# A routed transformer branch on one core: smaller pieces and another order in its preparation, mask, softmax and MLP

## The chip, the cores and the metric

One core of one Trainium2 chip. The metric is the device time of one execution in microseconds, of which the median of several runs is given. Lower is better.

## What is computed

Two layers on x of 2048 x 128, all in float32. Each is `x + s * silu(g)`, with s an attention and g a second branch, both of the layer-normed x. The change is in layer 0's second branch, the routed one, and in what prepares it. Cut to what matters:

```python
def _L0_ffn_ref(x, attention_mask, position_ids, router_w, router_b, wq, wk, wv, wo, w1, w2, ln1, ln2):
    weights = (x @ router_w)[..., 0] + router_b[0]
    k = int(CAP * s)                                  # 256 of 2048
    topv, topi = jax.lax.top_k(weights, k)
    sel_mask = (weights > topv[:, -1][:, None]).astype(x.dtype)
    kc = k - 1                                        # 255
    sel_idx = jnp.sort(topi[:, :kc], axis=1)
    x_sel, pos_sel, w_sel = x[bidx, sel_idx], position_ids[bidx, sel_idx], weights[bidx, sel_idx]
    m_sel = m[bidx[:, :, None], sel_idx[:, :, None], sel_idx[:, None, :]]   # 512 x 512 mask, indices clamped
    hn = rmsnorm(x_sel, ln1)
    q, kk, v = rope(heads(hn @ wq), pos_sel), rope(heads(hn @ wk), pos_sel), heads(hn @ wv)   # 16 heads of 8
    a = jax.nn.softmax(q @ kk.T / sqrt(8) + m_sel, axis=-1)
    x1 = x_sel + (a @ v).reshape(...) @ wo
    x2 = x1 + jax.nn.gelu(rmsnorm(x1, ln2) @ w1) @ w2
    proc = x2 * w_sel[..., None]
    out = jnp.zeros_like(x).at[bidx, sel_idx].set(proc)
    return out + x * (1.0 - sel_mask)[..., None]
```

The first attention (16 heads of 8, relu weights) and the whole second layer are not touched.

## The kernel before

Each stage is a block in which the five engines have a program of their own, written out by hand and tied by counting semaphores. An engine runs its instructions in the order written and stops at each `wait_ge`. At the end of a block all engines meet, and the next block starts. The stages are `prepare` (to 44.8 us in the profile), `routed0` (to 120.8 us), `attention0`, `between` and `attention1`.

`prepare` loads and norms x, turns it, makes the router's weights as a row and a column, projects q, k and v, and counts for each token how many weigh more. VectorE compares a weight column with the weight row for t = 0 to 15 (lines 258 and 261). ScalarE counts the first seven of these (line 295) and copies v after the first four. GpSimd makes rows of equal weights (lines 198 and 202) and TensorE adds the counts (lines 353 and 355). In between, `high(n)` on ScalarE copies a projected piece of q or k in TensorE's own rounding (line 287), and `low(n)` on VectorE makes the rest of it (line 252). `HIGHS_AFTER` and `LOWS_AFTER` say behind which t; n = 0 to 3 is q, n = 4 to 7 is k. SyncE stores each of the four parts to DRAM, 1 MB apiece, when its pieces are there (line 166), and the block can't end before these have landed. The first attention reads q and k back from there.

`routed0` gathers the chosen tokens by matmuls with one-hot rows, made by VectorE from the ranks (line 877), last 12 row tiles first and then the four tiles of the 512 tokens that the mask covers (`T_ORDER`). GpSimd adds up the 12 later tiles (`tails`, lines 865 to 868), since the mask takes all later tokens as its last one. VectorE squares and norms the gathered rows (lines 889 to 901), TensorE turns and projects them. The mask is taken by columns (`mask_columns`, line 1063, copies on line 1010) and then by rows (line 1129), and copied to `mask_sel` (line 941). Scores of four heads at a time (`score`) are masked by VectorE (line 955, two halves of 128 slots a head), exponentiated by ScalarE (line 1026), turned by TensorE (line 1148) and weighed (line 1157). Behind that, in order: the reciprocal of the sums spread to all columns (line 965) and turned (1172), `place` of the one-hot rows (turned tiles, line 1077, copied on lines 1036 and 978), `oT` (969), output projection (1179), x1 (971), norm, w1 (1193), gelu (1040), w2 (1199), x2 (981), the scatter (1208) and silu (1044). Banks of PSUM are assigned by hand in `PLACE_BANK` and `TURN_BANK`. An activation function that is not in the loaded table costs ScalarE a table load (ACT_TABLE_LOAD).

Of the kernel before, what the change touches and what calls it, by code (L numbers as in the profile page):

```python
# [78 lines left out]
def prepare(nc, a, sh):  # L79

    with ExitStack() as ctx:
# [63 lines left out]
        HIGHS_AFTER = {2: range(NC, 2 * NC)}  # L145
        LOWS_AFTER = {1: range(0, 2), 2: range(2, NC), 10: range(NC, 2 * NC)}
# [561 lines left out]
def routed0(nc, a, sh):  # L708


    with ExitStack() as ctx:
# [106 lines left out]
        PLACE_BANK = [0, 1, 2, 3, 2, 3, 5, 6]  # L818
# [27 lines left out]
        def _(pool):  # L846
# [17 lines left out]
            pool.wait_ge(ranked, T - MT)  # L864
# [6 lines left out]
        def _(dve):  # L871
# [65 lines left out]
            for i in range(RES):  # L937
                nc.vector.tensor_scalar(qm[:, i, :], bank[6][:, 0:SLOTS], head_rows[:, i:i + 1], None,
                                        ALU.mult).then_inc(qm_done, 1)
            dve.wait_ge(mask_taken, 1)  # L940
            link(nc.vector.tensor_copy(mask_sel[:, :, 0:SEL],
                                       bank[7].rearrange("p (s k) -> p s k", s=NS)[:, :, 0:SEL]))
# [7 lines left out]

            for n in range(H):
                if n % GH == 0:
                    dve.wait_ge(scored, n // GH + 1)
                for s in range(NS):
                    last = nc.vector.tensor_tensor_reduce(
                        out=prob[:, head(n), s, :], in0=bank[n % GH][:, s * SLOTS:(s + 1) * SLOTS],
                        in1=mask_sel[:, s, :], scale=-1.0, scalar=3.0e38, op0=ALU.add, op1=ALU.min,
                        accum_out=top[:, head(n), s:s + 1])
                last.then_inc(masked, 1)
                if n % GH == GH - 1:  # L960
                    for m in range(n - GH + 1, n + 1):
                        if not by_act(m):
                            take_probs(m)
            dve.wait_ge(exped, H)
            nc.vector.reciprocal(hn[:, :, :].rearrange("p s (h j) -> p s h j", j=HD0),
                                 total[:, :, :].unsqueeze(3).to_broadcast([P, NS, H, HD0])).then_inc(share_ready, 1)
# [8 lines left out]
            take_turned(1, bank[7])  # L975
# [5 lines left out]
            link(nc.vector.tensor_tensor(proc[:, :, :], bank[4][:, 0:NS * D].rearrange("p (s d) -> p s d", s=NS),  # L981
# [15 lines left out]
        def _(act):  # L997
# [10 lines left out]
            for n in range(2):  # L1008
                act.wait_ge(cols_taken, n + 1)
                nc.scalar.copy(mask_cols[:, 2 * n:2 * n + 2, :], sh.psum[:, 2 * n:2 * n + 2, 0:SLOTS])\  # L1010
                    .then_inc(cols_out, 1)
            act.wait_ge(qk_turned, 1)
            nc.scalar.copy(kT[:, :], bank[7][:, 0:SLOTS]).then_inc(kT_done, 1)

# [7 lines left out]
            for n in range(H + 2):  # L1022
# [7 lines left out]
                if n >= 2 and by_act(n - 2):  # L1030
                    take_probs(n - 2)
# [1131 lines left out]
```

## Time and profile before

| | us |
|---|---|
| Median of 3 runs | 1413.13 (1411.38 to 1413.79) |
| The profiled execution | 1410.19 |
| Its span, first to last instruction | 1408.2 |
| Preparation / routed branch | 0 to 44.8 / to 120.8 |
| TensorE busy | 1313.0 (93%) |
| VectorE busy | 1015.9 (72%) |
| ScalarE busy | 749.8 (53%) |
| GpSimd busy | 691.9 (49%) |
| Mean granted TensorE clock | 0.982 of full |

Times in the rows are microseconds from the first instruction of the profiled execution. PE is TensorE's matmuls, PEld its weight loads, DVE VectorE, ACT ScalarE, POOL GpSimd, SPq SyncE's queue. A float32 matmul shows as two instructions. Several equal instructions in a row are one row with their count (x4), and its duration runs from the first's start to the last's end. The bracket tells how long the engine was idle before and who released it. An end that overlaps the next start by about 0.1 us is usual.

### The profile page before, as it was taken

The numbers are of one execution on the slowest core, as the hardware profiler recorded it, in microseconds if no ns is written. First come the engines' busy times: TensorE is split into PE (matmuls) and PEld (weight loads), VectorE is DVE, ScalarE is ACT, GpSimd is POOL, SyncE is SP. The second block draws the span as 40 slices with busy tenths as digits, with TensorE's granted clock in tenths as the row PEclk, the third lists the DMA queues.
The fourth block names the chain that finished last, engine by engine and source line by source line (L and its number), as shares of the span: only waits on it lengthen the run. The fifth ranks groups of instructions, "written<-read, shape, count | busy, mean of one in ns | idle before, by whom it ended". The sixth has DMA issues, their size and how long they took to land.

```text
span 1408.2 us, 25489 instructions
## 1 busy us (share of the span) xinstructions
PE 1313.0 (93%) x9902; PEld 674.9 (48%) x9902; DVE 1015.9 (72%) x1495; ACT 749.8 (53%) x1200; POOL 691.9 (49%) x527
## 2 busy tenths in 40 slices
PE   5778999999999987989999999999999999999897
PEld 3654222222222245555555655555555555555554
DVE  7666888888888875776766766766766666766768
ACT  5275777877777774334444444444344344344343
POOL 4301060100100010558678678677677677777671
PEclk9799999999999999999999999999999999999999
DMA  2511320000000000000000000000000000000000
GB/s 98 160 74 51 111 47 1 1 1 1 2 1 2 2 1 1 1 1 1 1 1 1 1 1 1 1 1 0 1 1 1 1 1 1 1 1 1 1 16 16
DMA packets 18166, 21.50 MB, mean 15 GB/s; under 512 B 7785, under 2 KB 15873, under 8 KB 16513
## 3 DMA queue, kind: packets, MB, share of 16 engines
q1 hardware_dynamic: 18048, 19.88, 4.6%
q8 instruction: 81, 1.33, 0.4%
q14 instruction: 37, 0.30, 0.1%
HBM read 14.63 MB, written 5.24 MB: 14 GB/s over the span
## 4 chain that ended last, share of the span: by engine, by line
PE 43%; DVE 11%; ACT 3%; issue 1%; POOL 1%; DVEq 0%; POOLq 0%; ACTq 0%
PE psum L1810 13%; PE psum L1788 12%; DVE part_max L1952 4%; PE psum L1731 4%; DVE inv L1973 4%; PE psum L1791 3%; ACT prob L1895 3%; PE psum L1769 2%; PE psum L1718 2%; PE psum L1757 2%; PE psum L1709 1%; DVE z L1976 1%; PE psum L1711 1%; PE psum L1710 1%; PE psum L1736 1%
## 5 line engine op out<-in xcount | busy, mean ns | idle before, releaser
L1698 POOL TENSOR_TENSOR acc<-acc,prob 128x1024 f32<-128x1024 f32 (+3 forms) x250 | 492.8, 1971 | 87.4 <-ACT prob L1895 57.6
L1895 ACT ACTIVATE prob<-psum 128x1024 f32<-128x1024 f32 (+1 forms) x320 | 283.3, 897 | 353.8 <-PE psum L1791 346.4
L1952 DVE TENSOR_REDUCE part_max<-psum 128x2 f32<-128x1024 f32 (+2 forms) x320 | 336.7, 1063 | 170.0 <-PE psum L1731 85.6
L696 DVE TENSOR_SCALAR w<-psum 128x512 f32<-128x512 f32 x472 | 304.7, 686 | 59.0 <-PE psum L553 46.6
L647 ACT ACTIVATE w<-psum 128x512 f32<-128x512 f32 x552 | 294.2, 600 | 85.4 <-PE psum L553 84.8
L573 PE MATMUL psum<-w,v_cols 128*32 128x512 f32 x2048 | 274.1, 608 | 0.0
L1810 PE MATMUL psum<-prob,v_pair 128*64 128x512 f32 (+3 forms) x1280 | 250.2, 532 | 0.7 <-POOL prob L1666 0.7
L1788 PE MATMUL psum<-q_hi,k_hi 64*128 64x512 f32 (+3 forms) x640 | 139.0, 430 | 30.4 <-DVE part_max L1952 21.5
L1810 PEld LDWEIGHTS psum<-prob,v_pair 128*64 128x64 f32 x1280 | 87.4, 137 | 145.2 <-issue 134.2
L1731 PE MATMUL psum<-k_hi,q_hi 64*128 64x512 f32 (+3 forms) x640 | 132.5, 411 | 6.0 <-DVE part_max L1952 4.4
L1788 PE MATMUL psum<-q_lo,k_hi 64*128 64x512 f32 (+3 forms) x640 | 119.1, 368 | 0.0
L1788 PE MATMUL psum<-q_hi,k_lo 64*128 64x512 f32 (+3 forms) x640 | 119.1, 368 | 0.0
L1791 PE MATMUL psum<-max_rows,ones_r 64*128 64x512 f32 (+3 forms) x640 | 118.7, 366 | 0.0
L1973 DVE RECIPROCAL inv<-psum 128x512 f32<-128x512 f32 x31 | 103.9, 3352 | 16.5 <-PE psum L1757 16.5
L553 PEld LDWEIGHTS psum<-q_rows,k_rows 32*128 32x128 f32 x768 | 40.3, 181 | 154.0 <-ACT w L647 148.1
L397 POOL TENSOR_SCALAR xa<-xa,rstd_j,shift_j 128x128 f32<-128x128 f32 x16 | 6.9, 449 | 209.0 <-DVE shift_j L389 209.0
L1666 POOL TENSOR_SCALAR_AFFINE_SELECT prob<-prob 128x256 f32<-128x256 f32 x128 | 53.3, 423 | 110.9 <-ACT prob L1895 110.1
L553 PE MATMUL psum<-q_rows,k_rows 32*128 32x512 f32 x768 | 101.6, 493 | 0.1
L1788 PEld LDWEIGHTS psum<-q_hi,k_hi 64*128 64x128 f32 x640 | 61.4, 188 | 78.0 <-DVE part_max L1952 47.4
L1731 PEld LDWEIGHTS psum<-k_hi,q_hi 64*128 64x128 f32 x640 | 61.2, 187 | 77.6 <-issue 40.8
L1694 POOL TENSOR_TENSOR acc<-prob 128x1024 f32<-128x1024 f32 x23 | 54.9, 2385 | 43.2 <-ACT prob L1895 41.4
L573 PEld LDWEIGHTS psum<-w,v_cols 128*32 128x32 f32 x2048 | 40.6, 108 | 63.8 <-ACT w L647 53.5
(301 smaller groups left out, 1411.3 us busy)
## 6 DMA issues: line engine op xcount, KB each, us to landing
q_rows<-q_dram SPq DMA_DIRECT2D x12, 256.0 KB
k_rows<-k_dram SPq DMA_DIRECT2D x3, 1024.0 KB
q_dram<-parts SPq DMA_DIRECT2D x2, 1024.0 KB, 4.2
k_dram<-parts SPq DMA_DIRECT2D x2, 1024.0 KB, 6.6
x<-in_L_attn_x SPq DMA_DIRECT2D x4, 256.0 KB, 4.0
mask<-in_L_ffn_attention_mask SPq DMA_DIRECT2D x1, 1024.0 KB, 6.0
x_high<-q_dram SPq DMA_DIRECT2D x4, 256.0 KB
x_low<-k_dram SPq DMA_DIRECT2D x1, 1024.0 KB
```

What stands on the lines that cost most here:

```text
L553: last = nc.tensor.matmul(pair_bank[n % RING][i], k_rows[group][rows, kt * P:(kt + 1) * P], q_rows[group][rows, qc * C:(qc + 1) * C], star ...
L573: last = nc.tensor.matmul(out_bank[turn % 2][h * VW:(h + 1) * VW, :], v_cols[group][:, kt, h, :], w[:, s % WR, h, :], start=(kt == 0), sto ...
L647: nc.scalar.activation(w[:, s % WR, 2 * m + i, :], pair_bank[n % RING][i], ACT.Relu)\
L696: nc.vector.tensor_scalar(w[:, s % WR, 2 * m + 1, :], pair_bank[n % RING][1], 0.0, None, ALU.max)\
L1698: nc.gpsimd.tensor_tensor(sums, sums, prob[:, s % PR, :, q0:C], ALU.add).then_inc(summed, 1)
L1731: last = nc.tensor.matmul(to[:, m, 0:n], q_hi[HALF[m], i * P:(i + 1) * P], k_hi[hp % 2][HALF[m], c * C:c * C + n], start=True, stop=not di ...
L1788: nc.tensor.matmul(to[:, m, q0:C], left[HALF[m], keys], right[HALF[m], at], start=n == 0, stop=False)
L1791: last = nc.tensor.matmul(to[:, m, q0:C], ones_r[HALF[m], :], max_rows[HALF[m], at], start=False, stop=True)
L1810: last = nc.tensor.matmul(out_bank[HALF[m], q0:C], v_pair[hp % 2][:, kt, HALF[m]], prob[:, s % PR, m, q0:C], start=kt == 0, stop=kt == (qc ...
L1895: nc.scalar.activation(prob[:, s % PR, :, q0:C], unit_both[n % RING][:, :, q0:C], ACT.Exp, scale=SCALE)\
L1952: nc.vector.tensor_reduce(part_max[:, :, i, c], unit_both[n % RING][:, :, 0:cols], AX_X, ALU.max)\
L1973: nc.vector.reciprocal(inv[:, :], side_bank).then_inc(inv_done, 1)
```

## The change

- k's high parts are copied behind ScalarE's second count (was: third), its low parts made behind VectorE's eighth compare (was: eleventh).
- GpSimd starts the sums of later rows when all 16 one-hot tiles exist (was: the 12 later ones).
- The mask: kT is copied ahead of the mask's columns, these are copied one by one, and the rows are made in two halves in two banks, with the first scores between them. The first four heads are masked by halves.
- The softmax sums are inverted at 32 columns and then spread by a copy.
- ScalarE runs a square root on a spare element behind the last probabilities, so that the table is loaded there.
- Two `place` calls go ahead of the share's transposes, two behind the output projection with the rest; banks follow.
- w1, gelu and w2 go by halves; w2's two row halves sum into two banks.

```diff
-        HIGHS_AFTER = {2: range(NC, 2 * NC)}
-        LOWS_AFTER = {1: range(0, 2), 2: range(2, NC), 10: range(NC, 2 * NC)}
+        HIGHS_AFTER = {1: range(NC, 2 * NC)}
+        LOWS_AFTER = {1: range(0, 2), 2: range(2, NC), 7: range(NC, 2 * NC)}
...
-        PLACE_BANK = [0, 1, 2, 3, 2, 3, 5, 6]
+        PLACE_BANK = [0, 1, 2, 3, 0, 1, 7, 6]
...
-            pool.wait_ge(ranked, T - MT)
+            pool.wait_ge(ranked, T)
@@ def _(dve) @@
-            dve.wait_ge(mask_taken, 1)
-            link(nc.vector.tensor_copy(mask_sel[:, :, 0:SEL],
-                                       bank[7].rearrange("p (s k) -> p s k", s=NS)[:, :, 0:SEL]))
+            MASK_BANK = [bank[7], bank[6]]
...
+            for s in range(NS):
+                dve.wait_ge(mask_taken, s + 1)
+                link(nc.vector.tensor_copy(mask_sel[:, s, 0:SEL], MASK_BANK[s][:, 0:SEL]))
+                dve.wait_ge(scored, 1)
+                for n in range(GH):
+                    last = mask_scores(n, s)
+                    if s == NS - 1:
+                        last.then_inc(masked, 1)
             for n in range(H):
-                if n % GH == 0:
-                    dve.wait_ge(scored, n // GH + 1)
-                for s in range(NS):
-                    last = nc.vector.tensor_tensor_reduce(
...
-                last.then_inc(masked, 1)
+                if n >= GH:
+                    if n % GH == 0:
+                        dve.wait_ge(scored, n // GH + 1)
+                    mask_scores(n, 0)
+                    mask_scores(n, 1).then_inc(masked, 1)
...
-            nc.vector.reciprocal(hn[:, :, :].rearrange("p s (h j) -> p s h j", j=HD0),
-                                 total[:, :, :].unsqueeze(3).to_broadcast([P, NS, H, HD0])).then_inc(share_ready, 1)
+            link(nc.vector.reciprocal(total[:, :, :], total[:, :, :]))
+            nc.vector.tensor_copy(hn[:, :, :].rearrange("p s (h j) -> p s h j", j=HD0),
+                                  total[:, :, :].unsqueeze(3).to_broadcast([P, NS, H, HD0])).then_inc(share_ready, 1)
...
-            take_turned(1, bank[7])
+            take_turned(1, bank[5])
...
-            link(nc.vector.tensor_tensor(proc[:, :, :], bank[4][:, 0:NS * D].rearrange("p (s d) -> p s d", s=NS),
+            link(nc.vector.tensor_tensor(proc[:, :, :], sh.psum[:, 4:4 + NS, 0:D],
@@ def _(act) @@
-            for n in range(2):
-                act.wait_ge(cols_taken, n + 1)
-                nc.scalar.copy(mask_cols[:, 2 * n:2 * n + 2, :], sh.psum[:, 2 * n:2 * n + 2, 0:SLOTS])\
-                    .then_inc(cols_out, 1)
             act.wait_ge(qk_turned, 1)
             nc.scalar.copy(kT[:, :], bank[7][:, 0:SLOTS]).then_inc(kT_done, 1)
+            for c in range(MT):
+                act.wait_ge(cols_taken, c + 1)
+                nc.scalar.copy(mask_cols[:, c, :], bank[c][:, 0:SLOTS]).then_inc(cols_out, 1)
...
+            nc.scalar.activation(idle[:, :], sh.ones[:, 0:1], ACT.Sqrt)
             act.wait_ge(share_spread, 1)
...
-            act.wait_ge(hidden, 1)
-            nc.scalar.activation(gate[:, :], sh.psum[:, 0:2, :].rearrange("p b c -> p (b c)"), ACT.Gelu_apprx_tanh)\
-                .then_inc(gated, 1)
+            for n in range(2):
+                act.wait_ge(hidden, n + 1)
+                nc.scalar.activation(gate[:, n * C:(n + 1) * C], bank[2 + n], ACT.Gelu_apprx_tanh).then_inc(gated, 1)
@@ def _(pe) @@
             for c in range(MT):
-                last = mask_columns(c, MT - 1)
-                if c % 2:
-                    last.then_inc(cols_taken, 1)
+                mask_columns(c, MT - 1).then_inc(cols_taken, 1)
...
-            pe.wait_ge(cols_out, 2)
...
+            pe.wait_ge(cols_out, MT)
+            mask_slots(0)
             score(0)
+            pe.wait_ge(qm_done, RES)
+            mask_slots(1)
...
                 if n == 2:
-                    pe.wait_ge(qm_done, RES)
+                    pe.wait_ge(masked, GH)
...
+            for u in range(2):
+                place(u)
             pe.wait_ge(share_ready, 1)
...
-            for u in range(NC):
-                place(u)
             pe.wait_ge(oT_done, 1)
...
-            for u in range(NC, NC + 3):
+            for u in range(2, NC + 3):
                 if u == NC:
-                    pe.wait_ge(placed_by_act, NC)
-                if u == NC + 2:
-                    pe.wait_ge(share_out, 1)
+                    pe.wait_ge(placed_by_act, 2)
                 place(u)
-            turn_hn(1, bank[7])
+            turn_hn(1, bank[5])
             place(NC + 3)
+            pe.wait_ge(placed_by_act, NC)
...
-                last = nc.tensor.matmul(bank[f // 2][:, (f % 2) * SLOTS:(f % 2 + 1) * SLOTS], w1[:, f * P:(f + 1) * P],
+                last = nc.tensor.matmul(bank[2 + f // 2][:, (f % 2) * SLOTS:(f % 2 + 1) * SLOTS], w1[:, f * P:(f + 1) * P],
...
-            last.then_inc(hidden, 1)
-            pe.wait_ge(gated, 1)
-            for s in range(NS):
-                for f in range(FT):
+                if f % 2:
+                    last.then_inc(hidden, 1)
+            for f in range(FT):
+                pe.wait_ge(gated, f // 2 + 1)
+                for s in range(NS):
```

`mask_scores(n, s)` is the masking instruction of line 955, and `mask_slots(s)` the matmuls of line 1129 for one s, into bank 7 or 6.

## Rows read from the trace of the kernel before

**Rows 1.** SyncE's waits from 0 to 180 us: total, times, longest.

```profile
SPq L81 <- DMA k_dram<-parts: 6.2, 1, 6.2
```

**Rows 2.** Timeline, end of the preparation: start, us, engine, line, op, out<-in [idle before].

```profile
29.00 0.58 ACT L299 COPY v<-psum 128x512 f32<-128x512 f32 x1
...
30.66 1.39 DVE L261 TENSOR_SCALAR_CACHE_REDUCE prob<-g,xa 128x1152 bf16<-128x1152 f32 x1
...
31.62 2.07 ACT L287 CAST parts<-psum 128x512 fp32r<-128x512 f32 x4
...
33.72 4.50 SPq L166 DMA_DIRECT2D k_dram<-parts  x2
...
35.19 2.47 DVE L252 TENSOR_TENSOR parts<-psum,parts 128x512 fp32r<-128x512 f32 x4
...
42.53 0.17 PE L355 MATMUL psum<-minus_b,equal 128*128 128x1 bf16 x1
...
44.86 0.18 DVE L874 TENSOR_TENSOR rank<-counts,before 128x16 f32<-128x16 f32 x1 [4.54 <-PEq L81]
```

**Rows 3.** Timeline, one-hot rows, gather and GpSimd's adds.

```profile
46.01 8.86 PEld L1052 LDWEIGHTS psum<-xa,onehot 128*128 128x128 f32 x56 [3.40 <-DVE onehot L877]
...
50.65 3.48 POOL L865 TENSOR_TENSOR prob<-onehot 128x1536 f32<-128x1536 f32 x1 [1.54 <-DVE onehot L877]
...
50.75 3.53 DVE L877 TENSOR_SCALAR onehot<-iota,rank 128x256 f32<-128x256 f32 x1
...
54.21 1.80 POOL L866 TENSOR_TENSOR prob<-prob 128x768 f32<-128x768 f32 x1
...
56.89 0.76 POOL L868 TENSOR_TENSOR prob<-prob 128x256 f32<-128x256 f32 x1
...
57.79 0.44 DVE L884 COPY xs<-psum 128x274 f32<-128x274 f32 x1 [0.72 <-PE psum L1052]
...
58.82 0.17 DVE L893 TENSOR_SCALAR square<-square 128x2 f32<-128x2 f32 x1
```

**Rows 4.** Lines 877 and 1931, VectorE: duration ns min/median/max, first and last start.

```profile
L877 DVE TENSOR_SCALAR onehot<-iota,rank x16: 333/342/3530, 45.3 to 56.1; 128x256 f32<-128x256 f32 x16
...
L1931 DVE TENSOR_TENSOR xa<-xa,g x3: 692/1732/1916, 1334.1 to 1381.0; 128x512 f32<-128x512 f32 x3
```

**Rows 5.** Timeline, from the mask's columns to the first exponential.

```profile
67.77 0.58 ACT L1010 COPY w_heads<-psum 128x512 f32<-128x512 f32 x1 [0.28 <-PE psum L1063]
...
68.25 0.38 ACT L1013 COPY kT<-psum 128x256 f32<-128x256 f32 x1
...
72.50 0.69 DVE L941 COPY mask_sel<-psum 128x510 f32<-128x510 f32 x1 [4.73 <-PE psum L1129]
...
74.53 0.51 ACT L1026 ACTIVATE prob<-prob,top 128x256 f32<-128x256 f32 x1 [5.90 <-DVE top L955]
```

**Rows 6.** Timeline, from the softmax's end to x2.

```profile
95.16 1.75 DVE L965 RECIPROCAL hn<-total 128x256 f32<-128x256 f32 x1 [1.04 <-ACT prob L1026]
...
95.88 0.58 ACT L1019 COPY mask<-psum 128x512 f32<-128x512 f32 x1 [0.27 <-PE psum L1148]
...
98.34 1.97 PE L1077 MATMUL psum<-ident,onehot 128*128 128x128 f32 x16
...
100.79 0.42 DVE L971 TENSOR_TENSOR x_sel<-psum,xs 128x256 f32<-128x256 f32 x1 [1.82 <-PE psum L1179]
...
101.10 1.28 ACT L1038 ACT_TABLE_LOAD   x1
...
107.17 1.02 ACT L1040 ACTIVATE w_heads<-psum 128x1024 f32<-128x1024 f32 x1 [3.27 <-PE psum L1193]
...
110.33 0.42 DVE L981 TENSOR_TENSOR proc<-psum,x_sel 128x256 f32<-128x256 f32 x1 [2.86 <-PE psum L1199]
```

**Rows 7.** Windows at the first attention's start: length, TensorE busy (instructions), clock, DMA share, GB/s.

```profile
122.00:123.00 1.00, 0.77 (x4) 0.60 0.16 16
...
128.00:129.00 1.00, 1.00 (x8) 0.50 0.69 172
```

More of the change, by code:

```diff
@@ L949, in take_probs, with mask_scores @@
                     .then_inc(probT_by_dve, 1)
-            for n in range(H):
-                if n % GH == 0:
-                    dve.wait_ge(scored, n // GH + 1)
-                for s in range(NS):
-                    last = nc.vector.tensor_tensor_reduce(
-                        out=prob[:, head(n), s, :], in0=bank[n % GH][:, s * SLOTS:(s + 1) * SLOTS],
-                        in1=mask_sel[:, s, :], scale=-1.0, scalar=3.0e38, op0=ALU.add, op1=ALU.min,
-                        accum_out=top[:, head(n), s:s + 1])
-                last.then_inc(masked, 1)
+            def mask_scores(n, s):
+                return nc.vector.tensor_tensor_reduce(
+                    out=prob[:, head(n), s, :], in0=bank[n % GH][:, s * SLOTS:(s + 1) * SLOTS],
+                    in1=mask_sel[:, s, :], scale=-1.0, scalar=3.0e38, op0=ALU.add, op1=ALU.min,
+                    accum_out=top[:, head(n), s:s + 1])
+            for s in range(NS):
[6 more added lines that the diff above has]
+                        last.then_inc(masked, 1)
+            for n in range(H):
+                if n >= GH:
[3 more added lines that the diff above has]
+                    mask_scores(n, 1).then_inc(masked, 1)
                 if n % GH == GH - 1:
@@ L1123, in score, with mask_slots @@
                 last.then_inc(scored, 1)
-            pe.wait_ge(cols_out, 2)
-            pe.wait_ge(kT_done, 1)
-            for s in range(NS):
-                for c in range(MT):
-                    last = nc.tensor.matmul(bank[7][:, s * SLOTS:(s + 1) * SLOTS], mask_cols[:, c, s * P:(s + 1) * P],
-                                            rows(c), start=(c == 0), stop=(c == MT - 1))
-            last.then_inc(mask_taken, 1)
+            def mask_slots(s):
+                for c in range(MT):
+                    last = nc.tensor.matmul([bank[7], bank[6]][s][:, 0:SLOTS], mask_cols[:, c, s * P:(s + 1) * P],
+                                            rows(c), start=(c == 0), stop=(c == MT - 1))
+                last.then_inc(mask_taken, 1)
+            pe.wait_ge(kT_done, 1)
+            pe.wait_ge(cols_out, MT)
+            mask_slots(0)
             score(0)
+            pe.wait_ge(qm_done, RES)
+            mask_slots(1)
             def wait_probs(n):
@@ L1192, in _ @@
             for f in range(FT):
-                last = nc.tensor.matmul(bank[f // 2][:, (f % 2) * SLOTS:(f % 2 + 1) * SLOTS], w1[:, f * P:(f + 1) * P],
+                last = nc.tensor.matmul(bank[2 + f // 2][:, (f % 2) * SLOTS:(f % 2 + 1) * SLOTS], w1[:, f * P:(f + 1) * P],
                                         hnT[:, :], start=True, stop=True)
-            last.then_inc(hidden, 1)
-            pe.wait_ge(gated, 1)
-            for s in range(NS):
-                for f in range(FT):
-                    last = nc.tensor.matmul(bank[4][:, s * D:(s + 1) * D],
+                if f % 2:
[3 more added lines that the diff above has]
+                for s in range(NS):
+                    last = nc.tensor.matmul(bank[4 + s][:, 0:D],
                                             gate[:, f * SLOTS + s * P:f * SLOTS + (s + 1) * P], w2[:, f, :],
```

## The prediction

> **What bounds the kernel now.** I read the page first: TensorE is busy for 93% of the span, but that is mostly the two attentions, which the edit does not touch. The edited code is all in the first 121 us. The chain of waits is of no use there (it is followed back only into the second attention), so I went to the timeline, stretch by stretch, and asked what each engine's first instruction after an idle time had waited for. Up to 121 us every stage hands its result to the next and nothing overlaps the attention behind it, so a microsecond taken off this chain is a microsecond off the kernel, as long as the attention keeps its pace.
>
> Four places matter. (1) The preparation ends when its last engine does. TensorE's last count ends at 42.70, but the next stage starts at 44.86: SyncE sits 6.2 us on the landing of the stores to k_dram, and all wait for it [rows 1, 2]. (2) In the one-hot stretch VectorE loses time to GpSimd: the 14th one-hot row takes 3.53 us where the median is 0.34; it starts 0.1 us after GpSimd's first add (50.65) and ends 0.15 us after it (54.13) [rows 3, 4]. (3) Scores wait for the mask: TensorE, ScalarE's copies, TensorE again, one VectorE copy of both halves, and only then the first masked score [rows 5]. (4) Behind the softmax come a reciprocal of 1.75 us, sixteen placing transposes between the last weighing and the output projection, a table load that the root waits for, and a gelu of 1.02 us in one piece [rows 6].
>
> **k's stores.** The high copies of k move from behind ScalarE's third count to behind its second, which with its value copy ends at 29.58. The four copies, 2.07 us, then end near 31.65 in place of 33.69, if their projection is done by then. VectorE's low parts go ahead of three compares: the eighth compare ends near 32.05, the low parts take 2.47, so they end at 34.5 instead of 37.66 [rows 2]. By the later store the landing moves 3.1 us; if the two share the bandwidth and the first sets the pace, 2.0. SyncE's wait began at 38.2, behind its last issue, so the landing was at 44.4; it comes to between 41.3 and 42.4, before TensorE's 42.70. TensorE's counts wait for GpSimd's equality rows and for compares that end when they did. So the landing stops being last and TensorE becomes last, and behind it stands the barrier, which took 0.4 us after the landing (44.4 to 44.86) [rows 1, 2]. The next stage starts near 43.05: **1.8 us gained**, bounds 1.2 (landing late) and 2.1.
>
> **The sums of later rows.** I keep the clock of before here. With GpSimd quiet the last three one-hots pass by 51.6, and TensorE, which was busy with the first 56 gather matmuls up to 54.9 anyway, finishes the other eight near 56.1, so that the copy of the gathered rows starts there and not at 57.79: 1.7 us seem won. But GpSimd's four adds now start at 51.7, not at 50.65, and take as long as before, 7.0 us (the third under 0.9): to 58.7 [rows 3]. VectorE's next work, the squares, reads two operands in SBUF. What such an instruction does beside a GpSimd add is shown by line 1931: 0.69 us alone, 1.73 and 1.92 while adds run [rows 4]; and one VectorE instruction gets through at each gap between adds, as the 14th one-hot did [rows 3]. So: gathered rows copied from PSUM 56.1 to 56.5; the first square waits for the second add, 57.06; the second square for the third, 57.95; the small scaling of the squares for the fourth, about 58.9. Before it started at 58.82 [rows 3]. **Gain 0**, bounds -0.2 and +1.2. The +1.2 is the case in which squares are not held: then the small scalings alone are held, and the sum matmul, which needs the fourth add at 58.7, stands ahead of the turned hn in TensorE's queue and caps it.
>
> The Trainium skill (SBUF — State Buffer, section "SBUF: two separate sides") says that the port pair which VectorE and GpSimd share is locked for a whole instruction, also by a VectorE instruction with two SBUF inputs beside a GpSimd one that reads SBUF. By that rule the squares are held and this edit gives 0, where the one-hots alone would promise 1.7; the trace of line 1931 agrees (0.69 against 1.92 us).
>
> **The mask by halves.** kT is copied first, while TensorE still makes the last columns; the four column copies of 256 take 0.38 each (as kT), and only the last one stands behind the last column, where a copy of 0.58 and then kT's stood: ready near 68.15 instead of 68.63, gain 0.5. TensorE then takes from 68.7 to 72.5 for both halves. Now it does one, near 1.9 us, then score(0), then the other, while VectorE masks the first half under it. The last half ends near 72.9; copy 0.42, one masked score, and the first exponential starts at 73.9 instead of 74.53 [rows 5]. **0.6 gained**, bounds 0.2 and 1.1 (whether score(0) holds TensorE for its whole time). ScalarE then paces the sixteen heads as before, two exponentials of 0.5 us each; the new wait for four masked heads ahead of the third head's transposes is long met, since ScalarE needs 3 us to get there.
>
> **Softmax to scatter**, in times of before [rows 6].
> - The reciprocal has 32 columns instead of 256: 0.22 in proportion, with a fixed cost up to 0.4; the copy spread to 256 columns 0.33 to 0.42 (a one-hot row, kT's size). About 0.8 for 1.75, ready at 96.0. But TensorE has place(0) and place(1) first, half of what took 1.97, so until 96.5. The share's transposes, which came behind 96.91, start at 96.5.
> - ScalarE loads the square root's table right behind its last probability copy (96.46): 1.28, and a tiny activation of 0.2, to 97.95. Only then comes the share copy, 0.37, to 98.3. The weighing, done by 98.34 before, is done at 97.9. So the table load takes back part of what the reciprocal gave.
> - oT takes 98.3 to 98.75 and the output projection follows at once; before, all sixteen placing transposes (98.34 to 100.1, where the next matmul gets in) held TensorE. With 0.75 for the projection x1 starts at 99.55 instead of 100.79: 1.25 gained.
> - Squares are ready 1.2 later (as from 57.79 to 58.99 [rows 3]), 100.75. Before, the root stood behind a table load that ended at 102.38; that load is gone, but two placing copies of 0.5 stand ahead on ScalarE and end near 101.1. Root at 101.1 instead of 102.4: 1.3 gained.
> - w1's eight matmuls have half the number and twice the columns of w2's sixteen, which take 2.1 (gelu's end 108.19 to 110.33). The first four give their half of the gelu 1.0 sooner: it starts near 104.9, takes 0.6, the second half ends at 106.45. w2's first half runs beside it from 105.6, its second from 106.6 and 1.1 more: x2 at 107.8 instead of 110.33. **2.5 gained in all**, bounds 1.5 and 3.0. VectorE's four placing copies stay hidden beside the gelus; uncovered they would cost 0.6 each.
>
> Sum: 1.8 + 0 + 0.6 + 2.5 = 4.9. The profiled execution took 1410.19 (span 1408.2 and 2.0 around it), so it would take 1405.3. The median of the runs shown, 1413.13, is 2.9 above it; for a median I say 1413.13 - 4.9 = **1408.2**.
>
> **The rivals.**
> - Squares not held by the adds: 1.2 more, 1407.0. For it: the squares are another form than line 1931, and none stands beside an add in this trace. Against: line 1931. Chance 0.10.
> - The clock at the start of the first attention. TensorE idles before 120.9, and the granted clock is at its low level (1.2 GHz) from 122.4 to 129 [rows 7]. At most half of such a stretch is lost, about 3 us. The shifted stage may be spared it: 1405.2. Chance 0.08.
> - Half the gain: the barrier still waits for the landing of two stores back to back, or ScalarE's queue with table load and placing copies sets the end of the branch. 4.9 less 1.2 to 2.5 leaves 2.4 to 3.7, that is 1409.4 to 1410.7, and with the spread of the runs mostly within 0.2% (2.8 us, about what a measurement of this kernel can tell from no change). Chance 0.18.
> - Slower: the same low clock lasts longer. It has to give back 4.9 + 2.8 = 7.7 us, at a half lost over 15 us more at the low level in the attention's first steps, more than twice the stretch of before. For it: the work in front of it moves by 5 us. Against: TensorE is busy all through. With 20 us more: 1418. Chance 0.04.
> - The main case keeps 0.60, its own range 1406.2 to 1410.0.
>
> Faster 0.60 + 0.10 + 0.08 = 0.78, same 0.18, slower 0.04. The range goes from the spared clock stretch, 1404.8, to the half gain with the runs' spread, 1411.4.
>
> **What would show it.** The routed stage starts near 43.0 with TensorE's count as the last of the preparation; the adds end near 56.9 and a square of over 0.5 us stands among them; the first exponential comes 2.4 us before 74.53; the square root's table load stands ahead of the share copy; two gelus; the attention's first matmul near 116.0. Wrong would be: squares of 0.29 us beside adds, SyncE still last, a share copy that isn't delayed, or another length of the low clock behind the attention's start.

## The result and the profile after

| | before | after |
|---|---|---|
| Median of 5 runs each, same comparison, us | 1411.38 (1410.73 to 1413.79) | 1403.77 (1402.92 to 1404.42) |
| Ratio | | 0.9942 [0.9928, 0.9955] |
| Profiled execution / its span | 1410.19 / 1408.2 | 1403.8 / 1401.9 |
| Mean granted TensorE clock | 0.982 | 0.986 |
| Attention's first matmul (L553) | 120.86 | 116.63 |

The kernel became faster, 7.6 us by the medians where 4.9 were forecast, and 1403.77 lies 1.0 below the range. The median of before was 1413.13 in three runs and 1411.38 in five, so 1.75 of the miss of 4.4 lies in the base of the sum. In the profiled executions 4.2 us were won ahead of the attention (120.86 to 116.63), 2.1 behind it, in code that the edit doesn't touch.

SyncE's waits of after [rows 1]: total, times, longest.

```profile
SPq L81 <- DMA k_dram<-parts: 6.4, 1, 6.4
SPq L81 <- PEq L81: 1.8, 1, 1.8
```

The timeline of after, end of the preparation [rows 2].

```profile
29.56 0.58 ACT L299 COPY v<-psum 128x512 f32<-128x512 f32 x1
30.02 2.07 ACT L287 CAST parts<-psum 128x512 fp32r<-128x512 f32 x4
...
32.12 3.47 SPq L166 DMA_DIRECT2D k_dram<-parts  x2
...
32.55 2.47 DVE L252 TENSOR_TENSOR parts<-psum,parts 128x512 fp32r<-128x512 f32 x4
...
43.62 0.19 PE L353 MATMUL psum<-one_b,prob 128*128 128x1 bf16 x1 [1.34 <-issue]
...
44.13 0.18 DVE L874 TENSOR_TENSOR rank<-counts,before 128x16 f32<-128x16 f32 x1 [3.24 <-PEq L81]
```

SyncE finds the stores landed at about 42.0 (its last issue ends at 35.59, then 6.4) and waits 1.8 more, for TensorE. The landing isn't last any more. But TensorE's last two counts stand behind a pause of 1.34 that nothing in the profile explains. The stage begins 0.73 earlier than before, not 1.8. A part of this arises ahead of the edit: from VectorE's first norm (L220) to its copy of the weight column (L243) after took 10.34 us and before 9.87.

The timeline of after, from GpSimd's first add to TensorE's sum of the later rows [rows 3].

```profile
50.97 3.44 POOL L865 TENSOR_TENSOR prob<-onehot 128x1536 f32<-128x1536 f32 x1 [2.59 <-DVE onehot L877]
...
54.44 0.44 DVE L884 COPY xs<-psum 128x274 f32<-128x274 f32 x1 [3.45 <-PE psum L1062]
54.49 1.81 POOL L866 TENSOR_TENSOR prob<-prob 128x768 f32<-128x768 f32 x1
54.92 1.53 DVE L889 CUSTOM_DVE_ANT_0 hn<-xs 128x128 f32<-128x128 f32 x1
56.38 0.87 POOL L867 TENSOR_TENSOR prob<-prob 128x256 f32<-128x256 f32 x1
...
56.38 0.28 DVE L889 CUSTOM_DVE_ANT_0 hn<-xs 128x128 f32<-128x128 f32 x1
...
56.70 0.57 DVE L893 TENSOR_SCALAR square<-square 128x2 f32<-128x2 f32 x1
57.31 0.20 ACT L1009 ACTIVATE root_sel<-square 128x2 f32<-128x2 f32 x1 [11.94 <-DVE square L893]
57.33 0.72 POOL L868 TENSOR_TENSOR prob<-prob 128x256 f32<-128x256 f32 x1
...
58.10 0.70 PE L1080 MATMUL psum<-prob,ones 128*128 128x256 f32 x2 [0.88 <-POOL prob L868]
```

The first square takes 1.53 us in place of 0.28 and ends just behind the second add (56.45 and 56.30). The second square follows in the same gap and isn't held. The tiny scaling is held (0.57) by the third add. The fourth add is waited for by TensorE's sum of the later rows alone (58.10), which ends before the normed rows are there to be turned (59.11), so it costs nothing here.

The timeline of after, mask [rows 5].

```profile
64.86 1.67 ACT L1022 COPY w_heads<-psum 128x256 f32<-128x256 f32 x4
...
66.67 1.53 PE L1135 MATMUL psum<-onehot,w_heads 128*128 128x256 f32 x6 [0.55 <-ACT w_heads L1022]
...
68.56 1.15 PE L1129 MATMUL psum<-kT,wo 32*128 32x256 f32 x16
...
69.64 1.56 PE L1135 MATMUL psum<-onehot,w_heads 128*128 128x256 f32 x6
...
71.67 0.42 DVE L957 COPY mask_sel<-psum 128x255 f32<-128x255 f32 x1 [0.32 <-PE psum L1135]
...
72.60 0.51 ACT L1035 ACTIVATE prob<-prob,top 128x256 f32<-128x256 f32 x1 [6.07 <-DVE top L950]
```

Both halves and score(0) stand one behind the other on TensorE, 66.67 to about 71.6.

The timeline of after, softmax's end to x2 [rows 6].

```profile
93.69 0.35 DVE L974 RECIPROCAL total<-total 128x32 f32<-128x32 f32 x1 [1.04 <-ACT prob L1035]
94.08 0.30 DVE L975 COPY hn<-total 128x256 f32<-128x256 f32 x1
...
95.01 1.28 ACT L1041 ACT_TABLE_LOAD   x1
...
96.30 0.20 ACT L1041 ACTIVATE idle<-ones 128x1 f32<-128x1 f32 x1
96.41 0.35 ACT L1043 COPY share<-psum 128x256 f32<-128x256 f32 x1
...
98.03 0.42 DVE L981 TENSOR_TENSOR x_sel<-psum,xs 128x256 f32<-128x256 f32 x1 [0.80 <-PE psum L1191]
...
99.42 0.22 ACT L1048 ACTIVATE root_sel<-square 128x2 f32<-128x2 f32 x1
99.66 1.28 ACT L1051 ACT_TABLE_LOAD   x1
...
103.36 0.60 ACT L1051 ACTIVATE w_heads<-psum 128x512 f32<-128x512 f32 x1 [2.42 <-PE psum L1204]
...
106.10 0.42 DVE L991 TENSOR_TENSOR proc<-psum,x_sel 128x256 f32<-128x256 f32 x1 [1.59 <-PE psum L1211]
```

The reciprocal and its copy take 0.7 for 1.75. The share copy waits for the table load, as forecast: TensorE delivered the turned share at about 95.5, and ScalarE takes it at 96.41.

In a table, each stage from its own start, so that a shift ahead of it doesn't count:

| stage, us | before | after | gain | forecast |
|---|---|---|---|---|
| VectorE's first norm to L874 (k's stores) | 34.01 | 33.20 | 0.8 | 1.8 |
| L874 to the copy of hnT (one-hots, adds, norm) | 16.49 | 15.60 | 0.9 | 0 |
| rotation to the first exponential (mask) | 11.53 | 11.22 | 0.3 | 0.6 |
| exponentials to the reciprocal (heads) | 20.63 | 21.09 | -0.5 | 0 |
| reciprocal to x2 | 15.17 | 12.41 | 2.8 | 2.5 |
| attention's first matmul to the end | 1287.34 | 1285.27 | 2.1 | 0 |

The attention's gain goes with the clock. The heads' loss of 0.5 isn't explained: both executions have one stretch of 3.4 us at the low level among the heads. Windows of after at the attention's start [rows 7]: length, TensorE busy (instructions), weight loads, VectorE, ScalarE, GpSimd, granted clock, DMA share, GB/s.

```profile
119.00:120.00 1.00, 0.90 (x8) 0.37 (x10) 1.00 (x3) 0.99 (x3) 1.00 (x3) 0.90 0.12 49
120.00:121.00 1.00, 1.00 (x8) 0.00 (x0) 0.84 (x2) 0.34 (x1) 1.00 (x2) 0.50 0.57 172
...
122.00:123.00 1.00, 1.00 (x12) 0.20 (x8) 0.78 (x2) 0.78 (x2) 0.37 (x1) 0.50 1.16 262
```

Summed over such windows, the low level (0.50, that is 1.2 GHz of 2.4) lasts 3.4 us here and 6.8 before. Behind 110 us as a whole it lasts 29.9 us before, in stretches at 122, 562, 794, 1002, 1108, 1316 and 1402, and 22.6 after, at 119, 788, 997, 1102, 1311 and 1396. These are the same places in the code, some 5 us earlier; the one at 562 is missing and the first is half as long. Two more stretches of after, around 788 and 893 (length, TensorE busy, clock, DMA share, GB/s):

```profile
786.00:787.00 1.00, 0.00 (x0) 1.00 0.00 0
...
789.00:790.00 1.00, 1.00 (x6) 0.50 0.00 0
```

```profile
891.00:892.00 1.00, 0.00 (x0) 1.00 0.00 0
...
894.00:895.00 1.00, 1.00 (x10) 1.00 0.00 0
```

In both TensorE idles for a little under 2 us and then works on. The clock falls behind the first idle time and not behind the second.

### The profile page after: what moved, and what is told of

Read it like the earlier page. It is cut to its first block, busy times and chain, and to the rows that moved or that the text cites. A ratio compares the mean times of both kernels' runs of the same rounds, so it can differ in the third digit from the quotient of the medians.

```text
span 1401.9 us, 25496 instructions
## 1 busy us (share of the span) xinstructions
PE 1309.4 (93%) x9902; PEld 672.0 (48%) x9902; DVE 1012.3 (72%) x1497; ACT 750.4 (54%) x1204; POOL 692.1 (49%) x527
## 4 chain that ended last, share of the span: by engine, by line
PE 43%; DVE 11%; ACT 3%; issue 1%; POOL 1%; DVEq 0%; POOLq 0%; ACTq 0%
PE psum L1822 13%; PE psum L1800 12%; DVE part_max L1964 4%; PE psum L1743 4%; DVE inv L1985 4%; PE psum L1803 3%; ACT prob L1907 2%; PE psum L1781 2%; PE psum L1730 2%; PE psum L1769 2%; PE psum L1721 1%; DVE z L1988 1%; PE psum L1723 1%; PE psum L1722 1%; PE psum L1748 1%
## 5 line engine op out<-in xcount | busy, mean ns | idle before, releaser
L553 PEld LDWEIGHTS psum<-q_rows,k_rows 32*128 32x128 f32 x768 | 40.0, 181 | 153.8 <-ACT w L647 146.3
L553 PE MATMUL psum<-q_rows,k_rows 32*128 32x512 f32 x768 | 101.2, 493 | 0.1
(303 smaller groups left out, 1404.7 us busy)
```

Of the source, the lines that this page charges most:

```text
L553: last = nc.tensor.matmul(pair_bank[n % RING][i], k_rows[group][rows, kt * P:(kt + 1) * P], q_rows[group][rows, qc * C:(qc + 1) * C], star ...
```

## The experiments

Each is the kernel after with one edit or none (sums_vector_filled and sums_scatter_filled have more), 4 to 10 runs of it beside 10 to 26 of before; ratios are to these runs of before, with a 95% interval. Stages and spans are of its profiled execution, compared with the table's.

**1. after_again.** The kernel after once more.

> The changed kernel once more, unchanged. Of the 6.4 us between the two profiled executions 4.2 are there at the first attention's start; the other 2.1 appear where the granted clock is at its low level in one and not in the other (3.9 instead of 6.6 us of it at the attention's start, none instead of 3 us near 562). Theory A, the low stretches fall by chance: this execution shows them at other places or of other lengths, and the span differs from 1401.9 by 1 to 3 us. Theory B, they belong to the kernel: same places within 1 us, span within 0.5 us of 1401.9. Median for both: 1403.8 give or take 1.

1404.71, ratio 0.9963 [0.9951, 0.9976], span 1402.6, the attention's first matmul at 115.70. The same kernel gains 6.0 here. The preparation took 32.08 for 33.20, with no pause of TensorE ahead of the last counts where after has 1.34, and the low level behind 110 us lasted 30.1, as before. So the branch gives 5.2 us and the rest 0.4.

**2, 3. delay_short, delay_long.** GpSimd clears a spare tile behind the branch, so that the attention starts 1.5 or 3.0 us later.

```diff
+            pool.wait_ge(combined, NC)
+            nc.gpsimd.memset(onehot[:, 0:8, :], 0.0)
+            nc.gpsimd.memset(onehot[:, 8:9, :], 0.0)     # delay_long: 8:16
```

> The changed kernel with GpSimd kept at work for about 1.7 us more at the end of the routed branch, all engines waiting. If the rest of the kernel is a fixed length, the time rises by 1.7 us (1405.5). If the low clock stretches behind it depend on the moment at which the stages begin, their lengths or places change and the rise is off by 1 us or more either way.

> The same with about 3.3 us. Fixed length: 1407.1. Dependence on the moment: off by 1 us or more, and not by the same amount as with the short delay. A longer idle time of TensorE may also lengthen the low stretch at the attention's start: then both are above their sums.

1407.92 (0.9978 [0.9967, 0.9989]) and 1408.04 (0.9978 [0.9969, 0.9987]). The expectations had 1405.5 and 1407.1 for a rest of fixed length, so both runs are above, and twice the delay cost the same. Between x2 and the attention the two profiles have 12.01 and 13.50 us (10.53 in after), so the delay is paid in full there. But delay_short had two low-level stretches among its heads (22.96 us) and delay_long none (20.22), and behind 110 us the low level lasted 41.1 against 33.3 us: the stretches differ by more than the 1.5 us between the two. In both profiles the low level at the attention's start lasted 10.2 us, where the eleven others without spare matmuls have 3.4 or 6.8. So a longer idle time of TensorE ahead of the attention went with a longer low stretch, which the second expectation had named.

**4. k_stores_as_before.** k's parts at their old places.

```diff
-        HIGHS_AFTER = {1: range(NC, 2 * NC)}
-        LOWS_AFTER = {1: range(0, 2), 2: range(2, NC), 7: range(NC, 2 * NC)}
+        HIGHS_AFTER = {2: range(NC, 2 * NC)}
+        LOWS_AFTER = {1: range(0, 2), 2: range(2, NC), 10: range(NC, 2 * NC)}
```

> Only the placing of k's high and low parts goes back to that of before. My sum had 1.8 us for it; the two profiles show the routed stage's start 0.7 earlier, with all of the preparation 0.6 later from its first load on, so 1.3. Theory of the sum: the routed stage starts 1.3 later (near 45.4 or, counted from the first count on, the same), SyncE again waits about 6 us for the landing. Rival: the landing is hidden or not by other things and the start moves by less than 0.5 us.

1406.11, 0.9967 [0.9957, 0.9976]; preparation 33.92. Its timeline and SyncE's waits:

```profile
43.44 0.18 PE L353 MATMUL psum<-one_b,prob 128*128 128x1 bf16 x1 [1.70 <-issue]
```

```profile
SPq L81 <- DMA k_dram<-parts: 6.2, 1, 6.2
...
SPq L81 <- PEq L81: 0.2, 1, 0.2
```

Here the pause is longest, 1.70, and costs nothing: the landing ends behind it. What stands ahead of the edit varies too (9.3 to 10.5 us from the first norm to the weight column), so I count from the weight column (L243) to L874. With late stores that took 24.14 us (before, pause 0.78) and 24.16 (here, 1.70). With early stores it took 21.5 to 21.6 in the six profiles without a pause and 22.3 to 22.9 in the eight with one of 0.8 to 1.3. So this edit is worth 2.6 us without the pause and 1.3 to 1.8 with it, in one and the same code.

**5. sums_early.** GpSimd's adds start with twelve one-hots, as before.

```diff
-            pool.wait_ge(ranked, T)
+            pool.wait_ge(ranked, T - MT)
```

> Only GpSimd's start goes back: it adds when 12 one-hot tiles exist. My prediction gave this edit 0; the profiles show 0.9 to 1.0 us from the stage's start to the turned hn. Theory of the profile: the hn is ready 0.9 later and so is everything behind. Rival, that the gain came from the clock rising 4.0 instead of 5.6 us after the stage's start: then the time stays the same within 0.3, since the clock rises as early here.

1405.18, 0.9962 [0.9952, 0.9971]. L874 to hnT took 16.48, as before (16.49) and 0.9 over after, though the clock rose as early as in after (4.0 us behind L874): the rival is out, and the term is this one wait.

It isn't always 0.9. Of the eleven profiles in which GpSimd's adds wait for all 16 tiles, eight took 15.6 to 15.7; there the clock rose 4.0 to 5.6 us behind L874. In delay_short, reciprocal_spread and gelu_in_one_loaded it rose at 7.0 to 7.4, the gathered rows were copied 11.8 to 12.0 us behind L874 (after: 10.31), and the stage took 16.3. Timeline of delay_short, where lines stand 3 lower:

```profile
56.55 0.28 DVE L892 CUSTOM_DVE_ANT_0 hn<-xs 128x128 f32<-128x128 f32 x1
...
56.88 0.57 DVE L896 TENSOR_SCALAR square<-square 128x2 f32<-128x2 f32 x1
```

The squares missed the gap behind the second add. The first was held by the third add (55.75 to 56.48), the second passed in the gap behind it, and the scaling was held by the fourth. The edit then gives 0.2, near the forecast.

**6. sums_on_vector.** The four adds move to VectorE.

```diff
-            pool.wait_ge(ranked, T)          # and the four adds on nc.gpsimd
+            dve.wait_ge(ranked, T)           # on VectorE, behind the threshold
+            link(nc.vector.tensor_tensor(tails[:, :, :], onehot[:, MT:MT + 6, :], onehot[:, MT + 6:T, :], ALU.add))
...
             dve.wait_ge(gathered, 1)
```

> VectorE makes the four adds itself, in the 3.5 us that it idles between the last one-hot and the gather's end, and GpSimd does nothing then. If GpSimd's adds hold the squares (0.28 alone, 1.53 in the profile after), both squares take 0.28, the small scaling 0.17, and the turned hn comes 1.3 to 1.7 us earlier. If the holding is not the cause, no change, or a loss when the adds (about 3.1 us by the 128x512 adds of 0.69) end behind the gather.

1402.04, 0.9946 [0.993, 0.9963], span 1399.1. Timeline:

```profile
49.74 1.76 DVE L879 TENSOR_TENSOR prob<-onehot 128x1536 f32<-128x1536 f32 x1
51.53 0.96 DVE L880 TENSOR_TENSOR prob<-prob 128x768 f32<-128x768 f32 x1
...
54.46 0.29 DVE L889 CUSTOM_DVE_ANT_0 hn<-xs 128x128 f32<-128x128 f32 x1
...
55.22 0.20 ACT L1009 ACTIVATE root_sel<-square 128x2 f32<-128x2 f32 x1 [11.03 <-DVE square L893]
```

The adds cost half as long on VectorE (1.76 for 3.44), lie under the gather, and both squares take 0.29. L874 to hnT: 14.60, a whole us under after. Set beside kernels in which the clock rose at the same time the gain is 1.1 to 1.65: 1.1 here (after_again 15.72), 1.65 in sums_vector_filled (13.95 against 15.60), 1.1 in sums_scatter_filled (15.23 against 16.31). The held square was real.

**7. mask_as_before.** Column copies in pairs ahead of kT's, both halves of the mask ahead of score(0); VectorE keeps its new order.

```diff
             mask_slots(0)
-            score(0)
             pe.wait_ge(qm_done, RES)
             mask_slots(1)
+            score(0)
```

> Column copies in two pairs ahead of kT, and both halves of the mask ahead of the first scores; VectorE still masks the first four heads by halves. The profiles show 0.3 from the rope to the first exponential where my sum had 0.6, split as 0.5 for the copies and 0.1 for the halves. If the copies give 0.5 and the halves take 0.2 back, this kernel is 0.3 to 0.5 later at the first exponential (11.5 to 11.7 from the rope instead of 11.2); since only the last of four heads' first halves stands before the second, it can also be later than before (11.5). Rival: the order does nothing, 11.2.

1406.44, 0.9963 [0.9949, 0.9978]. Rotation to first exponential: 13.02, worse than before (11.53): the scores come last, and VectorE then masks four first halves (1.4 us) ahead of the second mask copy. The expectation had 11.5 to 11.7 and named a time above 11.5 as possible. This is no measure of the old code: here the halves come on VectorE alone.

**8. reciprocal_spread.** The reciprocal on 256 spread columns again.

```diff
-            link(nc.vector.reciprocal(total[:, :, :], total[:, :, :]))
-            nc.vector.tensor_copy(hn..., total...to_broadcast([P, NS, H, HD0]))
+            nc.vector.reciprocal(hn..., total...to_broadcast([P, NS, H, HD0]))
```

> Only the reciprocal goes back to 256 columns (1.75 us). Because two placings stand ahead of the share's transposes on TensorE and the table load ahead of the share copy on ScalarE, I expect only 0.4 of the 1.1 us to show at oT: 3.5 from reciprocal to oT instead of 3.1. Rival (the reciprocal is on the path with its whole length): 4.2.

1407.2, 0.9969 [0.9956, 0.9983]. Reciprocal to oT took 3.38 for 3.11, so 0.27 of 1.1 saved on VectorE reach the path (expected: 0.4); the table load holds the rest. The heads took 23.09 us, with two low stretches.

**9. no_early_sqrt.** The tiny root ahead of the share copy is left out.

```diff
-            nc.scalar.activation(idle[:, :], sh.ones[:, 0:1], ACT.Sqrt)
```

> Only the activation that loads the square root's table early is taken out. The share copy then comes 0.9 earlier, but the weighing still sets the output product, so 0.2 are won there; behind it the load stands ahead of the root once more, behind the placing copies, and costs 1.3 less the 0.4 that the root waited anyway. Sum: about 0.8 slower. Rival (ScalarE's queue was the limit, and the early load only moved the wait): no change.

1406.23, 0.9977 [0.9967, 0.9987]. Timeline:

```profile
95.17 0.37 ACT L1042 COPY share<-psum 128x256 f32<-128x256 f32 x1 [0.51 <-PE psum L1185]
...
97.50 0.42 DVE L981 TENSOR_TENSOR x_sel<-psum,xs 128x256 f32<-128x256 f32 x1 [0.80 <-PE psum L1190]
...
99.03 1.28 ACT L1047 ACT_TABLE_LOAD   x1
100.33 0.20 ACT L1047 ACTIVATE root_sel<-square 128x2 f32<-128x2 f32 x1
```

From x1 to the root 2.83 us for 1.39, but from the reciprocal to oT 2.90 for 3.11: the early load wins 1.44 and costs 0.21, 1.2 in all where 0.8 was expected. From the root to x2 it took 8.25 for 6.68. TensorE idled 2.31 us for the normed rows (after: 0.90), and a low stretch fell on w1's matmuls.

**10, 11. mlp_in_one, gelu_in_one_loaded.** One gelu for both halves of the hidden columns; the second with its table loaded ahead by a tiny gelu.

```diff
-            for n in range(2):
-                act.wait_ge(hidden, n + 1)
-                nc.scalar.activation(gate[:, n * C:(n + 1) * C], bank[2 + n], ACT.Gelu_apprx_tanh).then_inc(gated, 1)
+            nc.scalar.activation(idle[:, :], sh.ones[:, 0:1], ACT.Gelu_apprx_tanh)   # gelu_in_one_loaded only
+            act.wait_ge(hidden, 2)
+            nc.scalar.activation(gate[:, :], sh.psum[:, 2:4, :]..., ACT.Gelu_apprx_tanh).then_inc(gated, 2)
```

> Only the gelu goes back to one piece of 1024 columns (w1's and w2's orders stay). My sum had 1.2 us for the halves, the profiles show 1.25 between root and x2. Theory: root to x2 takes about 7.9 in place of 6.7, at the same clock, and everything behind comes 1.2 later. Rival: w2's new order of its own gives part of it, then less than 0.8.

> The gelu in one piece again, with a one-element gelu right behind the root so that the table is loaded there, as in the changed kernel. Theory: 8.0 from root to x2 instead of 6.7, if no low clock stretch falls into it (1.6 more if it falls on w2). Rival: most of the loss of the run before was the load's place; then under 7.3.

1408.28 (0.9976 [0.9965, 0.9986]) and 1405.14 (0.9952 [0.9937, 0.9967]). The timeline of mlp_in_one:

```profile
101.50 1.28 ACT L1050 ACT_TABLE_LOAD   x1 [4.63 <-PE psum L1204]
102.79 1.02 ACT L1050 ACTIVATE w_heads<-psum 128x1024 f32<-128x1024 f32 x1
...
103.86 3.67 PE L1211 MATMUL psum<-w_heads 128*128 128x128 f32 x16 [2.45 <-ACT w_heads L1050]
```

Root to x2 took 10.92 for 6.68, where 7.9 was expected. It measured three things at once: in this kernel the table load came behind the wait for the hidden columns (1.28), where in after it runs right behind the root (99.66), and w2's matmuls fell into the low clock (3.67 for 2.04), behind an idle time of 2.45. The second kernel has neither: root to x2 took 8.03 for 6.68, so halves are worth 1.35.

**12 to 14. filled_gaps, sums_vector_filled, sums_scatter_filled.** Spare matmuls of 512 columns, two behind the mask's second half and two behind the scatter, whose results nobody reads. The second kernel has the edit of sums_on_vector as well, the third too, but only the spare matmuls behind the scatter.

```diff
+            for _ in range(2):
+                nc.tensor.matmul(bank[7], sh.ident[:, :], sh.xnT[:, 0:C], start=True, stop=True)
```

> Two spare float32 matmuls of 512 columns (1.7 us) go into TensorE's idle time behind the mask's second half and two behind the scatter. Nothing waits for them. If idle time of TensorE brings on the low clock, the low stretches at 75.7 to 78.6 and at 119.9 to 123.9 are shorter or gone: up to 0.4 and 1.4 us. If they come on regardless, no change, or a loss of up to 0.5 where the spare matmuls end late.

> Both versions that came out below the changed kernel together: the sums on VectorE and spare matmuls in two of TensorE's gaps. The sums give 1.0 at the turned hn. If the spare matmuls keep the clock up, there is no low stretch between 70 and 85 and none at the first attention's start, again as in their own profile, and the time is near 1401 to 1402. If that profile was luck, low stretches stand there again and the time is that of the sums alone, 1402.0 to 1403.5.

> Sums on VectorE and the two spare matmuls behind the scatter, none behind the mask. If the spare matmuls keep the clock up there: no low stretch between 110 and 130 and the first steps of the attention at 1.44 us from the third on. If it was luck: a low stretch of 3.4 or 6.8 us there, as in 12 of 12 without them. Time 1401 to 1403.

1402.91 (0.995 [0.9931, 0.9968]), 1402.72 (0.9936 [0.9916, 0.9956]) and 1404.7 (0.9957 [0.9944, 0.9969]). The same windows, first of sums_vector_filled, then of sums_scatter_filled:

```profile
119.00:120.00 1.00, 1.00 (x12) 0.35 (x12) 0.68 (x2) 0.19 (x1) 1.00 (x2) 1.00 0.83 156
```

```profile
119.00:120.00 1.00, 1.00 (x8) 0.04 (x4) 0.83 (x2) 0.55 (x1) 1.00 (x2) 0.50 0.63 164
```

The spare matmuls cut TensorE's idle time ahead of the attention from 2.12 to 0.40 us. The first two profiles have no low stretch at the attention's start and looked like a cure; the third, with the same matmuls in the same gap, has one of 6.8 us. All 13 profiles without spare matmuls have such a stretch, two of three with them don't. Three profiles are too few to say that the gap ahead of the attention calls the low level.

## Why the prediction missed

**The step that failed** is the last one, from the sum to the median: "for a median I say 1413.13 - 4.9", with the clock kept as in before. The result lies 4.4 us under 1408.2. Of these 2.3 are the base (1413.13, where 71 runs of before have a mean of 1410.8). Another 1.5 are the clock: these five runs have a mean of 0.985 and the 71 have 0.9825, and a straight line through the 71 gives 0.6 us for each 0.001. The remaining 0.6 is the sum itself. In it the mechanisms held, with one exception. The step that was wrong there is "one VectorE instruction gets through at each gap between adds", which made the one-hot term 0; it measured 0.9. The ends of the range, 1404.8 and 1411.4, stand 0.4 and 0.7 outside of the rivals' own times (1405.2 and 1410.7), without a working.

**The base.** "For a median I say 1413.13 - 4.9". Three runs carried it. Over the 71 runs of before that stood beside all experiments the mean is 1410.8 (1407.65 to 1413.34), so the profiled execution's 1410.19 was the better base: 1410.19 - 4.9 = 1405.3, which I had written down and left, would have been 1.5 above the result.

**The sums of later rows: gain 0, measured 0.9.** The mechanism held up to one step. The adds started 6.84 us behind the stage's start, as forecast (51.7 - 44.86), took 7.1, and held a square. What failed is the line "one VectorE instruction gets through at each gap between adds": two did. The second square passed in the first square's gap, so the scaling waited for the third add and not the fourth. In the three profiles whose clock rose late, the squares came a gap later and the gain was 0.2. The rival "squares not held" is out. The trace agrees with the rule that I cited of the Trainium skill (SBUF — State Buffer, section "SBUF: two separate sides"), here with 1.53 against 0.28 us for the same instruction. How many get through in a gap I had read from one case.

**k's stores: 1.8, measured 0.8 and 1.9 over the whole preparation, 1.3 and 2.6 from the weight column on.** The landing came at 42.0, within the 41.3 to 42.4 forecast, and TensorE became last. Mis-sized was TensorE's end: 42.70 forecast, 43.84 measured, of which 0.58 is that everything ran later (the copy of v at 29.00 and 29.56), most of it from ahead of the edit, and 0.56 the longer pause (0.78 and 1.34). Where the pause was 0.81, nearly that of before (filled_gaps), the edit gave 1.8 from the weight column on (22.32 for 24.14), the forecast. after_again, without the pause, has 2.6. A wait that had covered an irregular pause was taken away, and the pause came out. My bounds had no term for it.

**The mask: 0.6, measured 0.3.** The copies gave 0.5 (they end 5.15 us behind the rotation's start, 5.63 before). The halves cost 0.2 instead of giving 0.1: TensorE needs 5.0 us from the first half to the end of the second, with score(0) and two pauses of 0.33 between, where I had 4.7. That is the low bound that I named, "score(0) holds TensorE for its whole time".

**Softmax to scatter: 2.5, measured 2.8.** oT 0.3, x1 1.0, root 0.2, MLP 1.25; the forecast had 0.2, 1.05 more, 0.05 more, 1.2. The table load took back most of the reciprocal, as costed. The next activation starts at 96.30, right at the load's end (95.01 + 1.28), and the copy ahead of the load ends at 94.99. The Trainium skill (ScalarE: Activation LUTs, section "What ACT_TABLE_LOAD costs") adds a drain of about 1.38 us to each switch; no row here shows one on either side of the load, and the measurement decides.

**The clock: forecast as a rival of 0.08.** I looked at one stretch only, the one at the attention's start. The sign that I had named for it came true (3.4 us at the low level for 6.8). Every profile here has 4 to 9 low-level stretches behind 110 us, and which of the recurring places are hit differs between two executions of one kernel (after and after_again). The time from the attention's first matmul to the end follows their sum, from 1283.79 us (filled_gaps, 19.7 us low) to 1290.39 (reciprocal_spread, 37.7). A straight line through all 16 profiles gives 0.28 us for each us at the low level (correlation 0.97); for the 7.3 us between before and after that is the 2.1 us won behind the branch. The prediction had taken a half as the most. The runs say the same without a profile. Eight runs of before had a mean clock of 0.985 and took 1408.96 in the mean; the five of after have the same mean clock and 1403.70. At 0.982, fourteen runs of before have 1411.04, the five of after_again 1405.45. So at an equal clock the edit gives **5.3 to 5.6 us**, close to the 4.9 and to what was measured in the branch (4.2 and 5.2). Of the 7.6 by the medians 1.5 are the better clock of these five runs, and the rest is that the five runs of before beside them stand a little above the mean of the 71. Whether the edit makes the better clock likelier can't be told: ten runs of after average 0.9835, 71 of before 0.9825. As far as the runs show, it was luck.

What TensorE did before the clock fell can be read from the rows. Between 110 and 1390 us TensorE idles for 1.0 us or more at 14 or 15 places in each profile, 237 in all (in quarters of a us). 94 of the 95 low stretches there begin 1.0 to 5.3 us behind the start of such an idle time; the 95th is that of sums_scatter_filled, behind the shortened gap. 143 of the idle times have no low stretch behind them. So idle time goes ahead of the fall, and which idle times are hit stays open.

## What to carry to other kernels

When a wait is taken off the end of a block, list what it covered: the next engine's end with its own irregular pauses decides, and takes its share of the gain. Where two engines use SBUF side by side, moving the smaller job to the engine that is free (VectorE did GpSimd's adds in half the time, under the gather) was better here than choosing whom to hold: sums_on_vector has the lowest median, 1402.04 of four runs (not told apart from the 1402.7 and 1402.9 of the next two), and is 1.0 us ahead of after in that stage, 1.1 to 1.65 where the clock rises at the same time. And before a gain of 0.2 to 0.5% is explained by the edit, set the runs beside each other at the same granted clock.

## What the hardware showed that I had not expected

- Ahead of the last one-column counts of the preparation TensorE pauses for 0.78 to 1.70 us in ten of the 16 profiles, with nothing to wait for in the profile, and not at all in the other six. With k's stores early the code there is the same in the eight profiles with a pause and the six without.
- The low level comes behind idle times of TensorE of 1.0 us and more (94 of 95 stretches), and behind fewer than half of these. Mostly it lasts about 3.4 us, at recurring places (788 to 794, 997 to 1002, 1102 to 1108), not at all of them in each execution. In the MLP it appears in the two kernels in which TensorE idles longest (2.31 and 2.45 us) and in no other. Among the heads the stage took 20.22 us without one, 20.6 to 21.7 with one (in gelu_in_one_loaded of 6.8 us) and about 23 with two.
- Two VectorE squares of 0.28 us get done about one gap between two chained GpSimd adds: the held one ends as the gap opens and the next follows. The add that they delay is lengthened too (0.87 for the 0.72 of its equal).
- Where a table load stands to the wait ahead of its activation differs: for the gelu it ran right behind the root, ahead of the wait, in 14 kernels (99.66 in after, 102.62 in before) and behind the wait in mlp_in_one (101.50), where it cost 1.28 us. What decides isn't shown. A tiny activation ahead of the wait had it loaded there (gelu_in_one_loaded).
